# A two-layer transformer on one core: a ring of four exponential steps, and the row-maximum transfers cut in four

## The reference

```
x = x + attn0(layernorm(x))      # one head, 64 wide
x = x + ffn0(layernorm(x))       # 256 x 256, values rounded to fp8
x = x + attn1(layernorm(x))      # 16 heads of 16, rotary embedding
x = x + ffn1(layernorm(x))       # gated, mixes each row with the row before

# attn1, for each sequence and head
scores  = (rope(Q) @ rope(K).T) / 4      # causal
weights = softmax(scores, axis=-1)
out     = (weights @ V) @ W_O.T
```

## Time and profile before

| | |
|---|---|
| median of 3 runs | 2562.5 us (2561.86 to 2568.54) |
| the profiled execution, its own time | 2564.48 us |
| its span, first to last instruction | 2562.6 us |
| mean granted TensorE clock | 0.961 |
| PE, DVE, ACT, POOL busy | 89%, 78%, 59%, 21% |

### The profile page before, as it was taken

The page is one execution under the profiler, slowest core; times in us unless marked ns, Lnnn a source line. Parts: engine busy times, 40 slices in busy tenths (PEclk is TensorE's granted clock), DMA queues, the critical chain, the costliest instruction groups (busy, mean ns, idle before and its releaser), DMA issues.

```text
span 2562.6 us, 51736 instructions
## 1 busy us (share of the span) xinstructions
PE 2287.1 (89%) x19060; PEld 1051.6 (41%) x19060; DVE 1992.9 (78%) x4326; ACT 1512.8 (59%) x2753; POOL 528.7 (21%) x526
## 2 busy tenths in 40 slices
PE   6788878899999999999989999899999989998896
PEld 4444433343444444353434435344344434332344
DVE  4577688888877887879786787887887689889922
ACT  2235437666656657666655565666665567677762
POOL 4444110212114120220304213031211400000011
PEclk7899879999999999999999999999999999999998
DMA  1222211020312222030211302012021121110110
GB/s 47 80 80 71 68 47 43 27 68 17 81 33 50 66 56 60 22 85 12 66 38 37 95 23 80 25 37 70 17 73 33 39 68 45 30 44 23 27 44 27
DMA packets 184102, 125.37 MB, mean 49 GB/s; under 512 B 83120, under 2 KB 183600, under 8 KB 183856
## 3 DMA queue, kind: packets, MB, share of 16 engines
q1 hardware_dynamic: 183088, 121.16, 17.3%
q10 hardware_dynamic: 768, 0.92, 0.1%
HBM read 62.20 MB, written 59.24 MB: 47 GB/s over the span
## 4 chain that ended last, share of the span: by engine, by line
PE 54%; DVE 29%; ACT 6%; issue 5%; DMA 2%; SPq 1%; DVEq 1%; POOL 1%; POOLq 0%; ACTq 0%
DVE mx L1506 20%; PE psum L1815 11%; PE psum L1760 6%; PE psum L1793 5%; PE psum L1726 4%; ACT probs L1266 4%; PE psum L1599 3%; PE psum L1690 2%; PE psum L1846 2%; PE psum L1661 2%; PE psum L1866 2%; PE psum L1835 2%; PE psum L1747 2%; PE psum L1630 2%; DVE xn L1387 2%
## 5 line engine op out<-in xcount | busy, mean ns | idle before, releaser
L1266 ACT ACTIVATE probs<-psum 128x512 f32<-128x512 f32 x2176 | 1142.1, 607 | 506.1 <-PE psum L1793 297.0
L1506 DVE TENSOR_REDUCE mx<-psum 128x1 f32<-128x512 f32 (+2 forms) x2304 | 1285.6, 621 | 143.5 <-PE psum L1760 110.8
L1815 PE MATMUL psum<-probs,vs 128*17 128x512 f32 (+3 forms) x5120 | 592.7, 544 | 3.2 <-ACT probs L1266 2.2
L1760 PE MATMUL psum<-kst,qst 48*128 48x512 f16 (+3 forms) x2560 | 443.5, 356 | 95.7 <-DVE mx L1506 47.3
L1793 PE MATMUL psum<-qst,kst 50*128 50x512 f16 (+3 forms) x2560 | 434.7, 354 | 68.3 <-DVE mx L1506 28.0
L1760 PEld LDWEIGHTS psum<-kst,qst 48*128 48x128 f16 x2560 | 134.0, 94 | 409.4 <-DVE mx L1506 160.8
L1793 PEld LDWEIGHTS psum<-qst,kst 50*128 50x128 f16 x2560 | 130.0, 93 | 384.9 <-ACT probs L1266 150.9
L1815 PEld LDWEIGHTS psum<-probs,vs 128*17 128x17 f32 x5120 | 92.9, 96 | 163.1 <-issue 130.6
L1051 POOL TENSOR_SCALAR vare<-mv 128x4 f32<-128x4 f32 x64 | 15.9, 249 | 682.8 <-DVE mv L1368 682.8
L1767 PE MATMUL psum<-maskq,identh 64*128 64x128 bf16 (+1 forms) x2048 | 133.5, 207 | 0.0
L1080 POOL TENSOR_TENSOR sums<-probs 128x512 f32<-128x512 f32 x12 | 15.3, 1274 | 520.4 <-ACT probs L1220 520.4
(11 more groups left out here) (171 smaller groups left out, 2762.6 us busy)
## 6 DMA issues: line engine op xcount, KB each, us to landing
qk_dram<-parts SPq DMA_DIRECT2D x168, 128.0 KB
qst<-qk_dram SPq DMA_DIRECT2D x128, 96.0 KB, 2.4
kst<-qk_dram SPq DMA_DIRECT2D x128, 96.0 KB, 2.3
v_dram<-vst SPq DMA_DIRECT2D x64, 136.0 KB, 4.6
vs<-v_dram SPq DMA_DIRECT2D x64, 136.0 KB, 2.1
xs<-x_in SPq DMA_DIRECT2D x16, 512.0 KB, 4.1
x_dram<-xs SPq DMA_DIRECT2D x16, 512.0 KB, 2.9
att_dram<-ast SPq DMA_DIRECT2D x64, 128.0 KB, 2.0
```

Source lines behind the costliest of these rows:

```text
L1266: act.activation(dst, src, ACT.Exp, scale=DK1 ** -0.5 / LIFT ** 2).then_inc(S["exp"], 1)
L1506: ins = dve.tensor_reduce(mx1[:, n % 2, 2 * g + odd, tile % TPC, c:c + 1], bank(src, at, at + cols), AX.X, ALU.max)
L1760: ins = pe.matmul(two[odd][:, at:at + cols], qst[rows, qslot, pair, P * (tile % TPC):P * (tile % TPC + 1)], kst[rows, kslot, pair, 0:cols] ...
L1815: ins = pe.matmul(bank(7, off, CH, rows=VW, row=32 * h), vtile[:, h, :], probs[:, HG * (step_no(b, hg, k) % 2) + h, at:at + CH - off], sta ...
```

## The change

Three things. `probs` gets places for four steps instead of two (`PSTEPS`), so that an `exp` waits for the `values` four steps back. The order of the negated maxima in `nmaxb` becomes part, side, pair, tile instead of side, part, pair, tile: two reductions of 8 columns write `nmax1` side by side, then one scaling and one subtraction of 16 columns follow, in place of one reduction of 16, one scaling, and two subtractions of 8. With the part first, each part and side is 8 rows of `nmaxT1` that go to one partition of `qst`, by a transfer of their own: four of 1 x 8 x 128 for each block in place of two of 2 x 8 x 128. The planner's estimates for `nmax` and `rows` go from 0.54 to 0.8 and from 0.2 to 0.3. DVE also waits for its own `out` of the block before, ahead of the next reciprocal.

```diff
+PSTEPS = 4
@@ head_jobs
-        add("DVE", "nmax", me, end, 0.54, *[...], ("turnmax", old))
+        add("DVE", "nmax", me, end, 0.8, *[...], ("turnmax", old))
-        add("SP", "rows", me, end - 20, 0.2, ("turnmax d", me), lat=2.6)
+        add("SP", "rows", me, end - 20, 0.3, ("turnmax d", me), lat=2.6)
-            two = step_before(b, hg, k, 2)
+            two = step_before(b, hg, k, PSTEPS)
@@ build
-        probs = sb("probs", [P, 2 * HG, CH], F32)
+        probs = sb("probs", [P, PSTEPS * HG, CH], F32)
-        nmax1 = sb("nmax1", [P, HG, TPC], F32)
-        nmaxb = sb("nmaxb", [P, 2, MAXROWS, HG // 2, TPC], F16)
+        nmax1 = sb("nmax1", [P, 2, HG // 2, TPC], F32)
+        nmaxb = sb("nmaxb", [P, MAXROWS, 2, HG // 2, TPC], F16)
@@ rows, on SP
                     for odd in range(2):
-                        row = HALF * odd + PROWS
-                        sp.dma_start(qst[row:row + MAXROWS, n % QRING, :, :],
-                                     nmaxT1[16 * odd:16 * (odd + 1), n % 2, :]).then_inc(S[f"rows {n % QRING}"], 16)
+                        for row in range(MAXROWS):
+                            at = 8 * (2 * row + odd)
+                            sp.dma_start(qst[HALF * odd + PROWS + row:HALF * odd + PROWS + row + 1, n % QRING, :, :],
+                                         nmaxT1[at:at + 8, n % 2, :]).then_inc(S[f"rows {n % QRING}"], 16)
@@ exp, on ACT
-                    wt.job("values", step_before(b, hg, k, 2))
+                    wt.job("values", step_before(b, hg, k, PSTEPS))
-                    at = HG * (step_no(b, hg, k) % 2)
+                    at = HG * (step_no(b, hg, k) % PSTEPS)
@@ nmax, on DVE
-                    link(dve.tensor_reduce(nmax1[:, :, :], mx1[:, n % 2, :, :, 0:q + 1], AX.X, ALU.max, negate=True))
-                    minus = nmax1[:, :, :].rearrange("p (g o) t -> p o g t", o=2)
-                    link(dve.tensor_scalar(nmaxb[:, :, 0, :, :], minus, 1.0 / UNIT1, None, ALU.mult))
                     for odd in range(2):
-                        ins = dve.scalar_tensor_tensor(out=nmaxb[:, odd, 1, :, :], in0=minus[:, odd, :, :],
-                                                       scalar=1.0 / UNIT1, in1=nmaxb[:, odd, 0, :, :],
-                                                       op0=ALU.mult, op1=ALU.subtract)
+                        ins = dve.tensor_reduce(nmax1[:, odd, :, :], mx1[:, n % 2, odd:HG:2, :, 0:q + 1], AX.X, ALU.max,
+                                                negate=True)
+                    link(ins)
+                    link(dve.tensor_scalar(nmaxb[:, 0, :, :, :], nmax1[:, :, :, :], 1.0 / UNIT1, None, ALU.mult))
+                    ins = dve.scalar_tensor_tensor(out=nmaxb[:, 1, ...], in0=nmax1[...], scalar=1.0 / UNIT1,
+                                                   in1=nmaxb[:, 0, ...], op0=ALU.mult, op1=ALU.subtract)
@@ out, on DVE
                     wt.job("turnout", item)
+                    wt.job("out", block_before(b, hg, q, 1))
```

More of the change, by code:

```diff
@@ L518, in head_jobs @@
         end = pos - LEAD + UNIT * (q + 1)
-        add("DVE", "nmax", me, end, 0.54, *[("max d", (*unit, odd)) for unit in units for odd in range(2)], ("turnmax", old))
+        add("DVE", "nmax", me, end, 0.8, *[("max d", (*unit, odd)) for unit in units for odd in range(2)], ("turnmax", old))
         add("PE", "turnmax", me, end - 20, 0.07, ("nmax", me), lat=0.1, claim="P", mode="C")
@@ L833, in rows_written @@
             n = block_no(b, hg, q)
-            wt.wait_ge(f"rows {n % QRING}", 32 * (n // QRING + 1))
+            wt.wait_ge(f"rows {n % QRING}", 64 * (n // QRING + 1))
         def v_loaded(wt, b, hg, c):
@@ L1519, in _ @@
                     wt.job("turnmax", block_before(b, hg, q, 1))
-                    link(dve.tensor_reduce(nmax1[:, :, :], mx1[:, n % 2, :, :, 0:q + 1], AX.X, ALU.max, negate=True))
-                    minus = nmax1[:, :, :].rearrange("p (g o) t -> p o g t", o=2)
-                    link(dve.tensor_scalar(nmaxb[:, :, 0, :, :], minus, 1.0 / UNIT1, None, ALU.mult))
                     for odd in range(2):
-                        ins = dve.scalar_tensor_tensor(out=nmaxb[:, odd, 1, :, :], in0=minus[:, odd, :, :],
-                                                       scalar=1.0 / UNIT1, in1=nmaxb[:, odd, 0, :, :],
-                                                       op0=ALU.mult, op1=ALU.subtract)
+                        ins = dve.tensor_reduce(nmax1[:, odd, :, :], mx1[:, n % 2, odd:HG:2, :, 0:q + 1], AX.X, ALU.max,
+                                                negate=True)
+                    link(ins)
+                    link(dve.tensor_scalar(nmaxb[:, 0, :, :, :], nmax1[:, :, :, :], 1.0 / UNIT1, None, ALU.mult))
+                    ins = dve.scalar_tensor_tensor(out=nmaxb[:, 1, :, :, :].rearrange("p o g t -> p (o g t)"),
+                                                   in0=nmax1[:, :, :, :].rearrange("p o g t -> p (o g t)"), scalar=1.0 / UNIT1,
+                                                   in1=nmaxb[:, 0, :, :, :].rearrange("p o g t -> p (o g t)"),
+                                                   op0=ALU.mult, op1=ALU.subtract)
                     ins.then_inc(S["nmax"], 1)
@@ L1777, in _ @@
                     pe.transpose(home(kind, item).bitcast(BF16)[0:32, 0:P],
-                                 nmaxb[:, :, :, :, :].rearrange("p o r g t -> p (o r g t)").bitcast(BF16), identb[:, :]
+                                 nmaxb[:, :, :, :, :].rearrange("p r o g t -> p (r o g t)").bitcast(BF16), identb[:, :]
                                  ).then_inc(S["turnmax"], 1)
@@ L1815, in _ @@
                             ins = pe.matmul(bank(7, off, CH, rows=VW, row=32 * h), vtile[:, h, :],
-                                            probs[:, HG * (step_no(b, hg, k) % 2) + h, at:at + CH - off],
+                                            probs[:, HG * (step_no(b, hg, k) % PSTEPS) + h, at:at + CH - off],
                                             start=(kb == 0), stop=(kb == TPC * q + 2))
```

## The result

The changed kernel takes 2540.4 us (2534.64 to 2545.64, 4 runs), the kernel before 2565.5 us (2561.86 to 2568.67, 4 runs): a ratio of 0.9902, 95% interval 0.9874 to 0.993. The prediction was 2561 us with a range of 2544 to 2577. So 25 us went, where I had forecast 1.

What follows compares the result with a forecast made beforehand. PE's work and its 275 us of gaps were taken to make the time. Ring -3, turnmax -2, rows +4 and chain 0 sum to -1 us, from 2562.5 to 2561.5, given as 2561 us, range 2544 to 2577.

Steps and rivals of the forecast that it cites:

- The ring: Four places in `probs` end ACT's 39.4 us of waits for values; 8% of that reaches PE: -3 us (0 to -39).
- the order hardly uses the new room: Scores stand three steps ahead at 2 of 576 values, never four; so the ring's term stays near its low end.
- My first rival: Faster: the order before was held back by two places beyond the 45 visible waits; 13 us, total 2551; chance 0.16.
- The draw: A new order shifts PE's busy time by chance: 6 us standard deviation per order, 8.5 us between two.
- The chain: DVE's instructions for negated maxima: 0.08 us shorter to 0.14 longer each, 64 chains; 0 us (-2 to +3).
- The turnmax: PE's 27.1 us of waits for negated maxima shrink as the planner's 0.8 places it later: -2 us (-10 to +7).
- The rows: Four transfers instead of two on SP's queue land 1.23 us later, delaying first scores at nine blocks: +4 us (+1 to +11).
- The count of packets for the new form: A row transfer of 8 rows into 8 pieces runs on eight engines, one packet per engine in place of eight.
- The signs named ahead: Expected in the changed profile: ACT's value waits gone, its idleness moved to score waits, PE's exponential waits near 40 us.
- the sign of being wrong: PE's gaps changing by over 8 us in unrelated rows of maxima and scores would mean the new order made the time.
- the redundant waits that I had named and left alone: Up to 29 semaphore waits ahead of DVE's chain, named as making it late, with 35.7 us of DVE idle time.

Runs made afterwards that it cites:

- four series: Kernel before under four series of the planner's random numbers: 1, 0.9955, 1.0095, 1.0038; with four places in program and planner: 0.9925, 0.9918, 0.9984, 0.9938.
- one wait, order of before: Kernel before, order untouched, with one semaphore wait ahead of each chain of maxima in place of up to 29: 2513.8 us, ratio 0.9795.
- maxima and rows alone: The changed kernel with two places in `probs` instead of four, replanned; chain, row transfers and new estimates kept: 2579.2 us, ratio 1.0034.
- Series + 100000: Kernel before, replanned with the planner's random seed raised by 100000, plus the wait for `out`: ratio 0.9955 with two places, 0.9918 with four.
- the planned ring: Kernel before with four places in program and planner and the wait for `out`; maxima, rows and their estimates as before: 2548.1 us, ratio 0.9925.

## Why the prediction was wrong, by its own steps

**The ring: -3 us. Here it failed.** The price was made from ACT's 39.4 us of waits under the order of before, and for that order it was right: four places without a new plan gave 0. This step took the cost of the ring at a fixed order for its cost in a new one. The error was the sentence that "the order hardly uses the new room", drawn from 58 and 89 score jobs ahead of values two steps back. The counts were right and said nothing of the time. The gain came through the plan: about 21 us on the mean of four series, 19 in the one at hand (0.9925 of 2567.9), where the term had 3. My first rival, that the order before was held back by the two places, was the true one, at a chance of 0.16. Its price of 13 us was low, and the reason that I gave for it, copies held up behind a late exponential in ACT's queue, was not the cause: that would have paid under the order of before too. My reading, argued and not shown: a condition binds at each choice of the planner, also where the chip shows no wait afterwards, since the planner has already worked round it. The planner's clock fits this reading, with 13 to 28 us less at four places. It could have been read ahead of the forecast. The kernel before and the changed one differ by only 3.5 us there, since the second has the dearer estimates; the changed kernel planned again with two places shows 20.1.

**The draw: 6 us, 8.5 between two.** Too small by more than half. Four draws with two places have a standard deviation of 15 us. The five windows of one run that I took it from share one series of choices and are cut at fixed times; they don't show what another series would give. With 15 us the range of 2544 to 2577 was too narrow for an edit that redraws the order. How much of the 25 us is the draw of this one order stays open. The planner's new estimates don't explain them: they go with 1.0034 against 1 at two places and 0.9902 against 0.9925 at four, one slower, one faster, and the second within the intervals.

**The chain: 0.** Right as far as shown. Its two reductions take 0.28 us together, where I gave 0.3, and the whole chain 0.70 us as before. The order held fixed shows no cost.

**The turnmax: -2 us.** Right in sign, and low: the row fell by 6.4 us, to 20.7 at 18 places, where 25 was forecast; the range of the term holds it. The fall came with the order: at that order with the old chain the row is 21.0 us at 18 places.

**The rows: +4 us.** Each piece was right: 630 ns for an issue, 2.65 us for four against 2.5, waits at first scores of 3.4 us, six times against 4 us at nine blocks. As time it did not show: at a fixed order two transfers in place of four gave 1.8 us, within what the runs tell, so the term is neither shown nor refuted. The count of packets for the new form was right too: the changed kernel moved 1792 packets more (185894 against 184102), which fits 256 transfers of 16 packets, eight of data and eight of completion, in place of 128 of 18. The rule of the Trainium skill, "DMA: Bandwidth & Descriptors", Issuing engines are not separate DMA queues, that the sequencer's time is usually small relative to the DMA, agrees with the runs no better than before: 2.65 us of issuing in at most 3.83. That it costs little here because little waits behind it is argued, not shown.

**The signs named ahead.** No exponential waits for line 1820: right. ACT's idle time moves to its waits for scores: no, those fell by 4.6 us; it did so only at the order of before, by 29.7. PE's waits for exponentials near 40 us: 37.1. PE's busy time within 5 us of 2287: no, 2278.5. And the sign of being wrong, gaps that fall by over 8 us in rows that have nothing to do with the three places: gaps fell by 21.7. The idle time before PE's matmuls of maxima and scores (lines 1760 and 1793) fell from 164.0 to 151.4 us, by 12.6, of which waits for exponentials have 3.5; the turnmax has 9.1. So by my own sign it was the new order.

**What stays open.** Why an order planned with more room is better in detail. Counted in the planner's lists, scores stand two steps or more ahead at 54, 48, 49 and 45 of 576 values with two places, and at 75, 76, 85 and 74 with four. But three places have 75, 68 and 82, and the one with 75 gained nothing. So the count shows that the room is used, not that its use pays. In the profiles of the four pairs, gaps of PE fell by 6.8, 12.7, 22.5 and 14.1 us and its busy time by 6.8, 1.6, 3.4 and 13.1: mostly gaps, and which ones differs from series to series.

## What to carry to other kernels

Where a generated schedule sets the order, price a resource twice: at the order as it stands (build that kernel: it is one line), and replanned, over several random series, since the same kernel differed by up to 36 us between two of its four draws (0.9955 and 1.0095). Read the planner's own total first: it costs nothing, and it was shorter with more room in every pair that ran faster, and once in a kernel with three places that ran no faster. A condition relaxed in the planner was worth some 20 us here, and the same one relaxed on the chip alone nothing that the runs can tell. And when the trace shows an engine idle for its own queue, look at what stands there: the redundant waits that I had named and left alone were worth twice the whole change.

## What the runs showed that I had not expected

**Waits already fulfilled cost time.** In the trace of the kernel before, the 29 semaphore instructions ahead of the chain of block (0, 0, 3) start within 2.70 us, and the reduction follows 2.80 us after the first. The first 0.69 us of that lie under the reduction that is still at work, and the other 2.11 us are the idle time. Inside such groups, one instruction starts 98 ns after the other in the median (the run has 1088 in 64 groups; all are gone with one wait, which the reduction carries). At that price they take some 107 us of DVE's queue, an estimate. Leaving them out gave 52 us under one order and 36 us under the other, while the row for DVE's idle time had 35.7 and 31.2. So what they cost can exceed the idle time named "issue".

**PE's busy time is no constant of the work.** The same 19060 matmuls took 2270.7 us at a mean granted clock of 0.966 (one wait, order of before), 2278.5 at 0.964 (the changed kernel), 2287.1 at 0.961 (before) and 2299.4 at 0.955 (maxima and rows alone). In these four the clock was higher where the gaps were fewer, and busy time went beside them: 8.6 us beside 21.7 of gaps, 16.4 beside 34.5. That gaps set the clock is not shown. Series + 100000 with two places has more gaps than the kernel before (277.7 us), and 0.968 and 2272.8 us; the planned ring has 2280.3 us at 0.961. And one kernel's own executions differ as much: in one comparison the kernel before ran from 2556.6 us at 0.967 to 2573.9 at 0.956. What can be said is that a forecast from gaps alone leaves out a part, which was a tenth to a half of the change in span in these pairs of profiles.
